# The end of the attention phase in another order: routing behind the last division, one unit of the shared expert and the logits ahead of the last output projection

## What is computed

```python
h = state_space_kernel(x)                          # (8, 256, 512)
h = concatenate([h, txt], axis=1)                  # (8, 384, 512)
h = h + attention(layernorm(h), Wq, Wk, Wv, Wo)    # 16 heads, 4 key/value heads, rotary
x2 = layernorm(h)
scores = softmax(x2 @ gate_w.T)                    # 64 experts, the best 6 of each token
y = sum over the 6 of score * expert(x2)           # SwiGLU, inner width 352, at most 64 tokens an expert
shared = silu(x2 @ sw_gate) * (x2 @ sw_up) @ sw_down   # inner width 704
out = h + y + shared
```

## Time and profile before

| | us |
|---|---|
| three runs | 1427.5, 1435.67, 1418.71 |
| median of the runs | 1427.5 |
| the profiled execution, its own time | 1441.19 |
| its span, first to last instruction | 1439.4 |
| PE busy in it | 1247.1 (87%) |
| DVE, POOL, ACT busy | 747.1, 503.2, 417.8 |

### The profile page before, as it was taken

One profiled execution on the slowest core, in us unless ns is written; L12 is line 12 of the kernel. 1 busy time (PEld: TensorE's weight loads), 2 busy tenths in 40 slices (PEclk: granted clock), 3 DMA queues, 4 the chain that ended last, 5 costly groups with the idle time before them and its releaser, 6 DMA issues. The chain is left out here.

```text
span 1439.4 us, 23556 instructions
## 1 busy us (share of the span) xinstructions
PE 1247.1 (87%) x9192; PEld 798.8 (55%) x9192; DVE 747.1 (52%) x1667; ACT 417.8 (29%) x693; POOL 503.2 (35%) x453
## 2 busy tenths in 40 slices
PE   6263778889999999999898789999999999989995
PEld 5253534445555554546455778666666666656662
DVE  7994457666677878686864532332322223222221
ACT  2220314344445444445354411111111111111110
POOL 0000101111114444443557673334444543444444
PEclk9698669999999999999999889999999999999997
DMA  3024142312525251615165263999999999998983
GB/s 115 0 62 101 39 89 42 86 42 64 129 63 134 53 144 43 155 35 136 46 198 181 97 195 53 290 309 295 303 336 341 299 337 343 282 299 284 331 271 40
DMA packets 144310, 239.82 MB, mean 167 GB/s; under 512 B 64569, under 2 KB 84681, under 8 KB 144201
## 3 DMA queue, kind: packets, MB, share of 16 engines
q1 hardware_dynamic: 120360, 214.10, 46.7%
q0 software_dynamic: 23840, 24.23, 9.4%
HBM read 175.59 MB, written 38.90 MB: 149 GB/s over the span
## 5 line engine op out<-in xcount | busy, mean ns | idle before, releaser
L2063 POOL DMA_INDIRECT out_rows<-mo_y,mo_scatter_half x128 | 182.9, 1429 | 239.8 <-DMA out_rows<-mo_y,mo_scatter_half 152.2
L1404 DVE TENSOR_REDUCE at_maxes<-at_ps 128x1 f32<-128x384 f32 x384 | 196.3, 553 | 59.5 <-PE at_ps L947 51.6
L1171 ACT ACTIVATE bulk<-at_ps 128x1152 f32<-128x1152 f32 x128 | 144.5, 1129 | 252.8 <-PE at_ps L912 251.5
L1682 POOL DMA_INDIRECT slot_table<-at_toki,at_si x144 | 145.5, 1011 | 119.9 <-DVE at_maxes L1404 87.0
L70 PE MATMUL mo_ps<-arena_view,arena_view 128*117 128x384 f32 (+1 forms) x864 | 168.8, 344 | 1.1 <-PEq L570 1.1
L70 PEld LDWEIGHTS mo_ps<-arena_view,arena_view 128*117 128x117 f32 (+1 forms) x864 | 146.5, 179 | 14.6 <-issue 14.5
L947 PE MATMUL at_ps<-late_view,late_view 128*128 128x384 bf16 x384 | 117.5, 352 | 28.9 <-DVE at_maxes L1404 16.7
L903 PE MATMUL at_ps<-arena_view,arena_view 128*128 128x512 f32 (+1 forms) x576 | 114.9, 351 | 3.6 <-ACT arena_view L1256 2.1
L903 PEld LDWEIGHTS at_ps<-arena_view,arena_view 128*128 128x128 f32 x576 | 90.6, 193 | 36.1 <-issue 22.3
L947 PEld LDWEIGHTS at_ps<-late_view,late_view 128*128 128x128 bf16 x384 | 31.0, 98 | 138.5 <-DVE at_maxes L1404 103.0
L912 PE MATMUL at_ps<-arena_view 97*128 97x384 f32 x384 | 96.4, 360 | 8.3 <-DMA arena_view<-at_mrow 5.1
(11 more groups left out here) (222 smaller groups left out, 1771.8 us busy)
## 6 DMA issues: line engine op xcount, KB each, us to landing
bulk<-in_L_ffn_w_gate SPq DMA_DIRECT2D x32, 704.0 KB
bulk<-in_L_ffn_w_up SPq DMA_DIRECT2D x32, 704.0 KB
late_view<-in_L_ffn_w_gate SPq DMA_DIRECT2D x32, 704.0 KB
late_view<-in_L_ffn_w_up SPq DMA_DIRECT2D x32, 704.0 KB
arena_view<-arena_view SPq DMA_DIRECT2D x96, 192.0 KB
late_view<-in_L_ffn_w_down SPq DMA_DIRECT2D x32, 512.0 KB
bulk<-in_L_ffn_w_down SPq DMA_DIRECT2D x32, 512.0 KB
out_rows<-at_hr SPq DMA_DIRECT2D x8, 768.0 KB
```

Of the source, the lines that this page charges most:

```text
L1171: A.activation(PT[:, N % RING, :, :], ps[:, 0:NT, 0:SEQ], ACT.Exp, scale=float(HD) ** -0.5)\
L1404: V.tensor_reduce(maxes[:, half, s, h:h + 1], ps[:, raw_bank(a, u), 0:SEQ], AX.X, ALU.max, negate=True)\
L1682: G.indirect_dma_start(slot_table, bass.IndirectOffsetOnAxis(ap=si[:, e % 2, m:m + 1], axis=0), toki[:, e % 2, m // TOPK:m // TOPK + 1], N ...
L2063: G.indirect_dma_start(acc_halves, bass.IndirectOffsetOnAxis(ap=scatter_half[:, half, 2 * p + e:2 * p + e + 1], axis=0), y[:, p % 2, e, co ...
```

## The change

Nothing is added and nothing is left out: each engine has the same work, in another order, with two waits moved.

- PE: `logits(B - 2)` and `shared_unit(0)` come ahead of the whole last output projection; `places(B - 2)` after eight of its twelve pieces instead of after all; units 1, 2 and 3 ahead of the turning of the last sequence's rows (before: 1 and 2), and unit 5 ahead of its logits (before: 4).
- The first output unit of a sequence (s == 0) is cut in two: the matmuls over chunks 0 to 4 wait for one chunk less, and only the last three wait for chunk 5.
- ACT: three splits of `sw_down` ahead of `gate_exponentials(B - 2)`, and the first `silu_shared` ahead of `normalised2(B - 1)`.
- DVE: `routing(B - 2, 4)` and `5` directly behind the last division, 6 and 7 each one step earlier, the splits of `sw_down` between them, and the products of the shared expert behind.
- POOL: `places(B - 2)` ahead of `inverse_deviation2(B - 1)`, with nine scatters ahead of it instead of ten; the eighteen scatters of sequence B - 4 spread differently within the last iteration (`LAST_SCATTERS`).

```diff
-    def out_of_hidden(self, T, out, s):
+    def out_of_hidden(self, T, out, s, chunks=None):
         last = 3 * self.SC - 1
-        for n in range(last + 1):
+        for n in range(last + 1) if chunks is None else range(3 * chunks[0], 3 * chunks[1]):
...
-        LAST_SCATTERS = {6: (0, 3), 7: (3, 6), 8: (6, 9), 9: (9, 12), 12: (12, 15), 14: (15, 18)}
+        LAST_SCATTERS = {4: (0, 1), 6: (1, 4), 7: (4, 7), 8: (7, 10), 9: (10, 13), 10: (13, 15), 12: (15, 18)}
...
-        SCATTERED_LAST = 0
-        SCATTERED_FIRST = 10
+        SCATTERED_FIRST = SCATTERS // 2
...  shared_unit, s == 0
-                    pe.wait_ge(s_hi_done, SC * (i + 1))
-                    pe.wait_ge(s_lo_done, SC * (i + 1))
+                    pe.wait_ge(s_hi_done, SC * (i + 1) - 1)
+                    pe.wait_ge(s_lo_done, SC * (i + 1) - 1)
                     pe.wait_ge(w_lo, PIECES)
                     pe.wait_ge(h2_ready, NT * B)
                     wait(pe, so_ready, NT * i)
+                    shared.out_of_hidden(T, ps[:, out_bank(s), :], s, (0, SC - 1))
+                    pe.wait_ge(s_hi_done, SC * (i + 1))
+                    pe.wait_ge(s_lo_done, SC * (i + 1))
+                    shared.out_of_hidden(T, ps[:, out_bank(s), :], s, (SC - 1, SC)).then_inc(s_down_done, 1)
+                    return
...  PE, after the loop
-            for i in range(4):
-                project_out(B - 1, i, 0)
             logits(B - 2)
-            for i in range(4, 12):
+            shared_unit(0)
+            for i in range(8):
                 project_out(B - 1, i, i // 4)
-            shared_unit(0)
             places(B - 2)
-            shared_unit(1)
-            shared_unit(2)
+            for i in range(8, 12):
+                project_out(B - 1, i, i // 4)
+            for u in range(1, 4):
+                shared_unit(u)
             turn_x2(B - 1, 0, (0, 1))
             turn_x2(B - 1, 1, (0, 1))
-            shared_unit(3)
+            shared_unit(4)
             turn_x2(B - 1, 2, (0, 1))
             turn_x2(B - 1, 3, (0, 1))
-            shared_unit(4)
+            shared_unit(5)
             logits(B - 1, 0)
-            for u in range(5, 9):
+            for u in range(6, 9):
                 shared_unit(u)
...  ACT, after the loop
             logits_copied(B - 2)
+            for m in range(2 * KC, 2 * KC + 3):
+                weights_hi(m)
             gate_exponentials(B - 2)
-            for m in range(2 * KC, PIECES):
+            for m in range(2 * KC + 3, PIECES):
                 weights_hi(m)
+            silu_shared(0, 0)
             normalised2(B - 1)
-            silu_shared(0, 0)
+            hi_shared(0, 0)
+            silu_shared(0, 1)
             x2_copied(B - 1, 0, 0)
             x2_copied(B - 1, 1, 1)
-            hi_shared(0, 0)
-            silu_shared(0, 1)
+            hi_shared(0, 1)
             x2_copied(B - 1, 2, 0)
             x2_copied(B - 1, 3, 1)
-            hi_shared(0, 1)
-            logits_copied(B - 1, 0)
             silu_shared(0, 2)
             hi_shared(0, 2)
+            logits_copied(B - 1, 0)
+            silu_shared(0, 3)
             gate_exponentials(B - 1)
-            for c in range(3, SC):
+            hi_shared(0, 3)
+            for c in range(4, SC):
...  DVE, after the last divide
+            routing(B - 2, 4)
+            routing(B - 2, 5)
             residual(B - 1, 0, 0)
             row_statistics2(B - 1, 0)
-            routing(B - 2, 4)
+            routing(B - 2, 6)
+            for m in range(2 * KC, 2 * KC + 3):
+                weights_lo(m)
             residual(B - 1, 1, 1)
             row_statistics2(B - 1, 1)
-            routing(B - 2, 5)
+            routing(B - 2, 7)
+            for m in range(2 * KC + 3, PIECES):
+                weights_lo(m)
             residual(B - 1, 2, 2)
             statistics2(B - 1, NT - 1)
-            routing(B - 2, 6)
-            routing(B - 2, 7)
             mult_shared(0, 0)
+            slots(B - 2)
             lo_shared(0, 0)
-            slots(B - 2)
-            for m in range(2 * KC, 2 * KC + 3):
-                weights_lo(m)
-            mult_shared(0, 1)
-            lo_shared(0, 1)
-            for m in range(2 * KC + 3, PIECES):
-                weights_lo(m)
+            for c in range(1, 3):
+                mult_shared(0, c)
+                lo_shared(0, c)
             routing(B - 1, 4)
-            mult_shared(0, 2)
-            lo_shared(0, 2)
             routing(B - 1, 5)
...  POOL, after the last out_lo
-            scatter(B - 3, SCATTERED_LAST, SCATTERED_FIRST)
+            scatter(B - 3, 0, SCATTERED_FIRST)
+            places(B - 2)
             inverse_deviation2(B - 1)
             scatter(B - 3, SCATTERED_FIRST, SCATTERS)
-            places(B - 2)
```

## The result

The changed kernel takes 1438.1 us (median of 20 runs, 1425.8 to 1447.5), the kernel before 1427.6 us beside it (20 runs, 1418.7 to 1442.8). The ratio is 1.0067 with a 95% interval of 1.0034 to 1.0099. In two more sets it was 1.0091 (1.0057 to 1.0125) and 1.0039 (0.9998 to 1.0080, which just holds 1). So it is slower, by 6 to 13 us by these ratios and 8 to 15 us between the medians, and the 1412 us of the forecast lie far off. A ratio leaves out runs in a slower state that some executions show, and the medians here don't, so the one is not the quotient of the others.

The account below looks back on a forecast made before the run. PE's own work was taken as the bound, with 17.6 us of stands in the tail. The new timetable ended the output units at 880.9 instead of 896.4, gaining 15.5 us: 1427.5 - 15.5 = 1412.0 us, range 1402 to 1422.

Parts of the forecast that it names:

- 8.79 us wait in `slots`: DVE's wait for POOL's `places(B - 2)`, ahead of `mult_shared(0, 1)`; forecast to be gone.
- stand of 1.90 us: PE's idle time, twice, before an output unit that wants the last chunk; forecast to go.
- The order behind the transposes: PE from the last transposes at 800.3 to the output units at 824.8; claimed as where the gain lies.
- the new wait: ACT's `sw_down` splits ahead of the exponentials: loads land at 785, PE stands 7.9 us before the last transposes.
- rival A: The forecast itself: `sw_down` loads land within 782 to 788, gain 12.5 to 18.5 us; chance 0.48.
- rival C: Longer wait: `sw_down` loads land at 789.87, the upper bound, 4.9 us less gain, 1417 us; chance 0.18.
- first half: The tail up to the turning of the last rows, where the change was said to bring nothing.
- the cover behind the logits: Units 6 to 8 on PE hide DVE's routing 4 and 5 of the last sequence, at most 6.2 us.
- rival D: No change: late signals of PE at three later hand-overs cost 14 us, giving 1426 us; chance 0.10.
- The 3.1 us: Time lost in PE's units 15 to 26, 29.7 us where 26.6 is needed; kept unchanged in the forecast.
- E: Slower: ACT's splits hold up the last sequence's x2; break-even at a landing of 800.5, 1443 us at 816; chance 0.06.
- POOL's gather: At the experts' start: gather at 872, rows landed by 877, PE wanting them at 884, 7 us of cover.

Follow-up runs that it names:

- a_stores: Changed kernel with the last sequence's two stores issued only after ACT copied the last logits, in a set with posts on time: 1425.3 us, ratio 0.9989.
- a_oldscatters_c: Changed kernel with the last iteration's scatters spread as before, run again in a set with posts on time: 1426.9 us, ratio 1.0033.
- after_again: Changed kernel unchanged, run again for a second trace, with posts late: 1448.0 us, ratio 1.0091 to the kernel before.
- b_scatters: Kernel before with only the new spread of the last iteration's scatters: 1428.3 us, ratio 0.9985.
- a_three: Changed kernel with exponentials ahead of all splits, old scatter spread, last stores behind the last logits: 1410.1 us, ratio 0.9869; again with late posts 1428.1, 0.9939.
- a_stores_c: Changed kernel with the last sequence's stores behind the last logits, run again in a set with late posts: 1443.9 us, ratio 1.0087.

## Why the prediction was wrong

**Right.** PE fills 772 to 792.0 without a stand; one stand follows, and it is the landing of `sw_down`; DVE's 8.79 us wait in `slots` is gone; the three output units take 12.55 us in both sequences (13.2 summed), with no stand of 1.90 us; the expert phase is no shorter. The order behind the transposes is worth what was summed, if nothing comes in between: 22.5 us (a_stores) and 23.1 (a_oldscatters_c) with posts on time, for 24.5.

**Wrong, the first step: the new wait.** The landing was set at 785 between bounds of 776.8 and 789.87. It comes 24.7 us after the last exponential here (788.11 - 763.42), and 24.5 to 24.9 in the other traces of the changed kernel; on before's trace that is 788.4, just outside rival A's 782 to 788 and 1.5 us short of rival C's bound. From the landing to the transposes it is 16.2 us for the 15.3 summed: DVE's second three low halves alone take 3.26 us where 1.9 was taken. The prediction itself said that its first half "brings nothing"; it costs 4.3 us (40.9 for 36.6). Against an order without the wait it costs more: 7.9 us with posts on time (40.3 for 32.4), 6.2 with late ones (40.7 for 34.5), and 12.8 and 8.1 us of measured time in two sets. So the step that failed first is the term for this wait: the landing was 3.4 us too early and the chain behind it 0.9 us too short, and the sum was compared only with the kernel before, not with the same change without the wait. A rule of the Trainium skill ("DMA: Bandwidth & Descriptors", section on why a DMA increments its semaphore by 16) was the base of an estimate of 782 at the earliest, later than my lower bound: the trace agrees with its direction, and the 788 it did not give.

**Wrong, the second step: the cover behind the logits.** "Need at most 6.2 us, which units 6 to 8 cover": with a post 5.2 to 14.4 us late they don't. That is the mechanism of rival D, to which I gave 0.10. I had seen it in one row, put it down to heavy loads, and took it as hidden behind another wait. It takes 8.4 to 10.7 us here (32.9 to 35.2 for 24.5). Of the 8.4 us in the trace shown, 0.8 come up to unit 8, 2.5 are PE's stand for the mask, 2.8 are the nine short matmuls of `places`, issued in pieces, and 2.2 are units 9 to 11 at a granted clock of 0.50 at first. The cause of the late posts is open.

The trace of before had more of this than the one row. ACT, before:

```profile
859.43 0.49 ACT L1221 ACTIVATE arena_view<-at_ps 118x384 f32<-118x384 f32 x1 [19.35 <-remote]
```

It waits here for unit 15, which PE's rows have finished at about 852.6, 6.8 us earlier, and from 856 to 860 the DMA share is 0.01. The 3.1 us that the prediction kept as lost in the second sequence belong to it: with posts on time units 15 to 26 take 25.1 us and not 29.7.

**Left out: the spread of the scatters.** I quoted the edit and gave it no price. With it the last iteration is 54.5 to 56.1 us in six traces of the changed kernel and its variants with late posts; without it, it is 50.7 to 52.1 in seven traces with late posts. ACT of after_again at that place:

```profile
752.08 1.13 ACT L1175 ACTIVATE bulk<-at_ps 128x1152 f32<-128x1152 f32 x1 [0.38 <-issue]
...
757.32 1.13 ACT L1175 ACTIVATE bulk<-at_ps 128x1152 f32<-128x1152 f32 x1 [3.43 <-remote]
```

An exponential waits 3.43 us for scores that PE had finished at 754.1, while the store of the sums passes, and PE stands 2.94 us in turn. b_scatters, whose loop is the same, has 52.2 and the time of before; a_stores, with posts on time, has 50.7. So I take it for a late post that hits or misses, worth up to 4 us; it is not shown as a cost of the edit by itself, and what makes it hit is open.

**The sum.** 15.5 forecast, less 4.3, less 8.4 to 10.7, less some 3.9 of the last iteration (54.7 for 50.8): -1 to -3.4, so slower. The table's sums say the same, 2.5 us more on the mean of three. The rest up to the 8 to 15 us between the medians is not placed: behind the start of the experts the three traces of the changed kernel take 540.8 to 547.1 us and those of before 535.3 to 542.9. Five of these six have one stand of 4.8 to 8.0 us for DVE's copy of the turned rows, at different places; without it they take 535.8 to 539.1 and 535.3 to 537.2 us.

I had a rival on the other side, E, but as one wait long enough by itself, with its break-even at a landing of 800.5. The landing came nowhere near it; three losses of 4 to 11 us together did it: the first is under rival C's 4.9, the second under rival D's 14, and the third had no rival.

**The limit named last, POOL's gather,** had a cover of 7 us in the prediction. (Its sum for POOL's list slips by 0.2 us: 797.7 + 57.6 + 4.1 + 3.3 is 862.7.) With posts on time PE arrives first and stands 8.0 to 10.2 us in all five traces of variants of the changed kernel, 8.99 us in a_stores. There PE needs 72.6 us from the last transposes to the end of the output units, for 80.6 summed, and POOL's gather comes after 74.6 us, for 71.7. So with posts on time a tail faster than this needs POOL's list shortened first; that wasn't tried.

**What beats both kernels:** a_three, 1410.1 us for 1427.3 with posts on time, and 1428.1 for 1434.3 with late ones. Of its edits only the order of exponentials and splits is shown to gain.

## What to carry over

Before work that waits for a transfer is put ahead of a critical step in a queue, find the landing in the trace; if no row shows it, let the critical step go first: here that order alone was worth 12.8 and 8.1 us. Give every edit of a change a price, those called spreading too. A hand-over that once came late in a trace is a cost for each short cover that the new order relies on.

## What the runs showed of the hardware

What PE posts can be seen 2 to 14 us after the end in its own rows, while PE issues matmuls in pieces 0.7 us or a multiple of it apart. The ends of PE's rows are the profile's model, so a trace can't tell whether the signal is late or the matmul itself ends later than its row says; either way the next engine goes on late. Late posts came in all traces of the first pair and of three sets; in those of two others hardly a post was late, and one of these two ran on a chip that had shown them late before. It does not need DMA traffic (share 0.02 in a_stores_c), nor does full DMA traffic bring it about: in a_stores the DMA engines are full from 823 to 839 us, and PE's 144 matmuls of L70 from 833 run in 25.30 us without a stand. Windows and PE of a_stores:

```profile
831.00:835.00 4.00, 4.00 (x21) 3.55 (x20) 0.69 (x1) 0.00 (x0) 3.09 (x4) 1.00 1.04 349
835.00:839.00 4.00, 4.00 (x25) 4.00 (x24) 0.60 (x2) 1.01 (x2) 3.09 (x4) 1.00 1.08 311
```

```profile
833.32 25.30 PE L70 MATMUL at_ps<-arena_view,arena_view 128*118 128x384 f32 x144
```

The kernel before takes 1421 to 1427 us in the sets with posts on time and 1428 to 1434 in the others. I have no cause for it.
